# A transformer block on one core: the score matmuls of two pairs of heads grouped into three stretches in place of four

## What is computed

```python
x = x + 0.5 * ffn(layernorm(x), ...)      # shared + 8 routed SwiGLU experts, top 4, hidden size 341
x = x + attention(layernorm(x), W_qkv, W_out)   # 16 heads of 64, causal, 512 x 512 scores
x = x + 0.5 * ffn(layernorm(x), ...)

# attention
score = einsum("bihd,bjhd->bijh", q, k) / 64 ** 0.5
masked_score = score * mask + 1e30 * (mask - 1.0)      # mask = lower triangle
wmat = softmax(masked_score, axis=2)
out = einsum("bijh,bjhd->bihd", wmat, v).reshape(b, l, H * D) @ W_out
```

## Time and profile before

| | |
|---|---|
| median of 3 runs | 647.27 us (646.82 to 647.6) |
| the profiled execution | 647.71 us |
| its span, first to last instruction | 646.0 us |
| TensorE busy | 634.6 us (98%) |
| VectorE busy | 594.0 us (92%) |
| ScalarE busy | 563.2 us (87%) |
| GpSimd busy | 499.7 us (77%) |
| granted TensorE clock | 1.00 throughout |

### The profile page before, as it was taken

One profiled execution on the slowest core, in us unless ns is written; L12 is line 12 of the kernel. 1 busy time (PEld: TensorE's weight loads), 2 busy tenths in 40 slices (PEclk: granted clock), 3 DMA queues, 4 the chain that ended last, 5 costly groups with the idle time before them and its releaser, 6 DMA issues.

```text
span 646.0 us, 20994 instructions
## 1 busy us (share of the span) xinstructions
PE 634.6 (98%) x7860; PEld 419.2 (65%) x7860; DVE 594.0 (92%) x1654; ACT 563.2 (87%) x1092; POOL 499.7 (77%) x621
## 2 busy tenths in 40 slices
PE   7799999999999999999999999999999999999998
PEld 5476765666676576667657666766666666666665
DVE  4999789999999999999999999999999989789887
ACT  5999997999999899999889999998999997565655
POOL 4354686889899688999967889987898998473655
DMA  7900000689889186796746987772599776110000
GB/s 202 286 3 2 3 1 2 91 133 139 125 133 158 33 147 126 124 143 123 118 76 120 148 132 133 138 142 55 103 158 147 126 147 89 37 18 2 19 1 18
DMA packets 226489, 62.97 MB, mean 97 GB/s; under 512 B 213202, under 2 KB 225620, under 8 KB 226388
## 3 DMA queue, kind: packets, MB, share of 16 engines
q1 hardware_dynamic: 226388, 61.64, 54.6%
HBM read 7.87 MB, written 1.05 MB: 14 GB/s over the span
## 4 chain that ended last, share of the span: by engine, by line
PE 85%; DVE 10%; issue 2%; ACT 1%; DMA 1%; SPq 0%; DVEq 0%; ACTq 0%
PE bank L1185 25%; PE bank L1186 23%; PE bank L1187 23%; PE bank L1379 8%; PE bank L1342 4%; DVE probs L1884 2%; DVE glu L1788 2%; DVE glu L1793 2%; DVE xs L1823 1%; PE bank L1229 1%; DMA vl<-in_L_ffn_Ws 1%; PE bank L1277 0%; DVE ql L1599 0%; ACT glu L1525 0%; DVE vl L1599 0%
## 5 line engine op out<-in xcount | busy, mean ns | idle before, releaser
L1148 POOL TENSOR_TENSOR glul<-glu,gluh 128x512 f16<-128x512 f32 x191 | 218.6, 1165 | 80.8 <-ACT gluh L1546 80.5
L1152 POOL TENSOR_TENSOR paired<-probs,paired 128x512 f16<-128x512 f32 x160 | 184.4, 1164 | 28.4 <-ACT paired L1571 27.8
L1525 ACT ACTIVATE glu<-bank,tanh_scale 128x512 f32<-128x512 f32 x167 | 112.5, 679 | 38.4 <-PE bank L1187 36.4
L1563 ACT ACTIVATE probs<-probs,exp_bias 128x128 f32<-128x128 f32 (+3 forms) x256 | 130.4, 552 | 1.8 <-POOL exp_bias L1160 1.4
L1884 DVE CUSTOM_DVE_ANT_0 probs<-bank,causal,score_scale 128x128 f32<-128x128 f32 (+3 forms) x256 | 126.0, 544 | 1.5 <-POOL paired L1152 0.9
L1185 PE MATMUL bank<-w3h,gluh 128*128 128x128 f16 x708 | 124.2, 219 | 0.0
L1546 ACT ACTIVATE gluh<-glu 128x512 f16<-128x512 f32 x191 | 113.6, 621 | 12.0 <-DVE glu L1793 11.9
L1187 PE MATMUL bank<-w3h,glul 128*128 128x128 f16 x708 | 124.0, 219 | 0.0
L1186 PE MATMUL bank<-w3l,gluh 128*128 128x128 f16 x708 | 124.0, 219 | 0.0
L1788 DVE SCALAR_TENSOR_TENSOR glu<-glu,bank 128x512 f32<-128x512 f32 x167 | 113.3, 679 | 7.8 <-ACT glu L1525 7.4
L1793 DVE SCALAR_TENSOR_TENSOR glu<-glu,bank 128x512 f32<-128x512 f32 x167 | 114.7, 687 | 5.8
(11 more groups left out here) (227 smaller groups left out, 1611.5 us busy)
## 6 DMA issues: line engine op xcount, KB each, us to landing
pT<-paired SPq DMA_TRANSPOSE x160, 3.3
attention_raw<-in_L_attn_W_qkv SPq DMA_DIRECT2D x6, 256.0 KB, 5.1
xs<-in_L_attn_inputs SPq DMA_DIRECT2D x4, 256.0 KB, 4.4
vh<-in_L_ffn_W SPq DMA_DIRECT2D x6, 128.0 KB
pT<-in_L_ffn_W SPq DMA_DIRECT2D x6, 128.0 KB
out<-xs SPq DMA_DIRECT2D x3, 256.0 KB, 2.8
raw_more<-in_L_ffn_W SPq DMA_DIRECT2D x4, 128.0 KB
attention_raw<-in_L_attn_W_out SPq DMA_DIRECT2D x2, 256.0 KB, 6.3
```

Of the source, the lines that this page charges most:

```text
L1148: pool.tensor_tensor(glul[pair][:, :], g[:, :], gluh[pair][:, :], ALU.subtract).then_inc(glu_low)
L1152: pool.tensor_tensor(paired[n % PAIRED][:, 1, :], probs[n % PROBS][:, :], paired[n % PAIRED][:, 0, :], ALU.subtract).then_inc(probs_low)
L1525: act.activation(g[:, :], psum[b1.bank][:, :], ACT.Tanh, scale=tanh_scale[:, j:j + 1]).then_inc(tanh_made)
L1563: e = act.activation(pr[:, at:at + (qt + 1) * P], pr[:, at:at + (qt + 1) * P], ACT.Exp, bias=exp_bias[:, gp % 2, qt, head:head + 1], scale ...
```

## The change

The table of when scores are made now depends on whether the pair is even or odd. An even pair makes its steps 0 and 2 at its first unit step, and at its fifth its step 3 together with step 0 of the next pair. An odd pair makes its steps 2 and 3 at its third. So two pairs have three places with scores, each with two scores steps. The softening has a table of its own. Matmuls, tiles and instructions are the same in number and shape on every engine. All four `ORDER` strings are new throughout (every line differs); each has the same letters, each as often as before.

```diff
-SCORED_AT = {0: [0], 2: [2, 3]}
+SCORED_AT = [{0: [(0, 0), (0, 2)], 4: [(0, 3), (1, 0)]}, {2: [(0, 2), (0, 3)]}]
+SOFTENED_AT = [{0: [(0, 0), (0, 2)], 4: [(0, 3), (1, 0)]}, {2: [(0, 2)], 3: [(0, 3)]}]
...
         def scores(n):
-            gp, u = b * PAIRS + n // NU, n % NU
-            for of_unit in SCORED_AT.get(u, []) if 0 <= n < last else []:
+            p, u = n // NU, n % NU
+            for ahead_by, of_unit in SCORED_AT[p % 2].get(u, []) if 0 <= n < last else []:
+                gp = b * PAIRS + p + ahead_by
                 uses = [self.bank() for _ in range(2)]
...
-                    scored[b * last + n + of - u] = uses if len(units) == 1 else [uses[k]]
+                    scored[b * last + (p + ahead_by) * NU + of] = uses if len(units) == 1 else [uses[k]]
...
         def soften(n):
-            gp, u = b * PAIRS + n // NU, n % NU
-            if 0 <= n < last and u in SCORED:
-                tiles, units = SCORED[u]
-                units = [(b * last + n + of - u, of) for of in units]
+            p, u = n // NU, n % NU
+            for ahead_by, of_unit in SOFTENED_AT[p % 2].get(u, []) if 0 <= n < last else []:
+                gp = b * PAIRS + p + ahead_by
+                tiles, units = SCORED[of_unit]
+                units = [(b * last + (p + ahead_by) * NU + of, of) for of in units]
...
     "tensor": (
-        "FFBFFFFTzTFTTGNSgTNhhTTGSTTTThdThdhdhhGdTTShTdddhhdddTTTdhGThShTdTThdddRhdTTXhdhzdhTTddhgTdddhhhdhdd"
-        "hhhddddhhdhdhhxzhxdddkvhhvvddvhhqkhdqqhvdxqxkhwqqwhddwhvkwwqhdddwwqqhdvhwqkhwwwdxqqxvgwhwdhdwwqkhdww"
...
+        "FFTFzTFFFFBGNSgTTTNhhGTTSTThTTddTdhhGddhhSddTTTThhhTdddTdThGhhSTdThdTdTdddRhhXhzddTTdThhgddhTdhhhhhd"
+        "ddddddhhhhhhddxzhxdvkvdhhdvvddhhqqkhvddhqxqxhkddwqqhwvhwwddwqkqhwwhvdwqqkhhwwwddqqvwwgxxhhdwwdqqkhww"
...
```

More of the change, by code:

```diff
@@ L712 @@
     "gpsimd": (
[L713 to L717, removed]
@@ L718 @@
-        "ssssssssssssssfsssssssssssssssH"
+        "LLnLLLLsfLLssLEsssssnsEsssssssEsEsWWsWWYsssssssWWnsssfWWssssssssbbsnppbpbpppbsbppyppbbsuppbpsssbppps"
+        "sbubpsppssbbppupbppsbpfspbubsppppbssbnppupbbsspsppbybusspppssspsnuubssbypppbsspbppbsbspppbbssppupbps"
+        "sbpppubssbpppbbfuppppbsbssppubpssbpppbubsppnppbsssbpppybbsuppsspspnsssuybubsspppbbssspppbbpppbpbsspu"
+        "ppbbsppsfpsbupbsppbpsbpuppbssbppsspbubppppbbsspnuppbsssbpppbypusbpnssppssuybssbsuspppsfbbspppbbpsppb"
+        "spsbpupbpsppbsupbsbppsppbbusspppbssbpnbppsbuppbpspybpupbspsbppspsbbupsspppsssssussufssssssssnssyssss"
@@ L719 @@
+        "sssfssssssssssssssssssssssssssH"
     ),
     "tensor": (
-        "FFBFFFFTzTFTTGNSgTNhhTTGSTTTThdThdhdhhGdTTShTdddhhdddTTTdhGThShTdTThdddRhdTTXhdhzdhTTddhgTdddhhhdhdd"
-        "hhhddddhhdhdhhxzhxdddkvhhvvddvhhqkhdqqhvdxqxkhwqqwhddwhvkwwqhdddwwqqhdvhwqkhwwwdxqqxvgwhwdhdwwqkhdww"
-        "dqqwhwqkhdwwqwqhddwqhkwhwwxqxdwqhhdwwoqwhddwwqqhdhwhwwhdwhdhwwkvvvwwhxqxvdkhqqhvhddddkqohwqqhwwvhdww"
-        "qkhdwqqxgwvwwhxdwdqkhdddwwqqhvwhqwwkhwwddqqhhwwwxqxkhdwwqqhwhwddqkhwwddwqqhwowqhwddwqqhhxwwhwxhhwhwd"
@@ new lines @@
+        "ddddddhhhhhhddxzhxdvkvdhhdvvddhhqqkhvddhqxqxhkddwqqhwvhwwddwqkqhwwhvdwqqkhhwwwddqqvwwgxxhhdwwdqqkhww"
+        "whqqdddwwkhwwqqhwhwddqqkwhhwxwwxqqhdohwwdddwqqdhhwhwwwhddhhxkwwwxwvvvhwddvqqkhhdvqqhddkhowqqvwwhhdqq"
+        "kwwhvgdwwxqxhdqdwwwkhddwwqqhvhdwqwwkqhdhwwwqqdhwkhwwxqxqwhhwddwdwqqkdhhdwwwqqwohwddqqwhhwxwhhxwwhhdd"
+        "dkwwwhvvvvdwwdhqqkhhdvdqxqxkgohhwwdqqvwhddqqwwkhwwhvdwqqhwwdkhddwwwqqhvhwwxqqxkhwwhdwqqkdwwhdwhdwqqd"
+        "dhwwqqwkhwhdxwwqqxwwhohddqqwwwhhddhwdwhhhdwdwwkvvhvwvwxxqqkghhhdddvddqqkhowqqhwwvhwdqkwhqvhwdwwqxqxd"
@@ L729 @@
+        "whkwhwdwqqvhdwwwddqqkhwhhwdqqwwwdkhxqwhxqwwhddqqwwkhhddwwwqqhowdwhwdqqwhhwwdxghwwxdhhhwddhwddwwhhhdd"
+        "hhxhxdohhhhddddhddxhhhxddhddhhddhghdxhxdhhhddhhdhdhhddxhxddhdhhhddhhddhxhxddhhhhhhdddddxHxddd6"
     ),
     "scalar": (
-        "BlzCMMMNPPPPPNMhrhsPPPhssPPsPPhhMMshshAAhPPsAssshMMMhPsPPAsAhhPhAAPPssAAshPhsPPhlsshzQhPWZsshPPPWWhh"
-        "shrshsWshhhssWWWhhsshsslhhWzshskvhhssvvssvhhsskheeppshevpeespkpheeplephhsvpeypkehpeeupsshpevhpeeskph"
-        "pepsussephrvepephepskhepeupsseheppskheeppuhepepshsepkshepeeppuhshepesepplhyeupepsshephehpephhsusshss"
@@ L734 @@
[L734 to L738, removed]
@@ L739 @@
-        "hhhsshhshshlssyshhshssshhssshhhssshhhhssrhhhhssshhssshshsshhshssshhhhsssshhhsshhhsshsssH"
+        "lzCBMMMNPPPPNMhPhsrssPPPPhsPPMMhhsPshshAAAPPshsPhPhssMMMPsPAhhsAhAPshAAPPPAPsshlhhsWWzPPsZhsWPhhsPWh"
+        "hrssshhhssWsWWhhhWshsshlhQszshkvvsshhsvvhshssskheeevppphleepkhpeypeshpshevpepepkshuehpeeppvssehkphep"
+        "epesssvuprehepphsepsskehpuephsepepepkheepsuheppheeppksshheesppeuplsheephsspespyuephheepphsshehpshkss"
+        "suvvvhlsvyukehhpeepvphssekpehpepssepvehphepsekphvsepersuphepepekhpeepussphehvpepeukpeehhpepspsshepkh"
@@ new lines @@
+        "epeupseshhpepepeuskpheephsseppslephepepuehyshpehshpsepshsepshkhusvvvvlyhssukehheppvepssskeeepphhreps"
+        "psvehpepepkeehphupvepssshepepkhepeusshpvehpepepkehpehupepsskepephshsepeupehpepepkssehphueepsssplheep"
+        "hpepyepuhssepshheephushhplsyskvvhvvssskheeeusrhppvhpsskheeppeepsphepheepvkpeesvhhppuessspeehppkhuepe"
+        "sspvhepepepukheeshphpepsssekpheuphepseehpplepkyepehphuepssehpepepshueepsshhpeeeshppsprhhhssussshhhhu"
+        "sssshhhshsshhhsshsshhlhyssshhhsshhsssshrhhsshhshhhssshssshshhhshsshsshhhhsshhsshhhsssssH"
@@ L740 @@
     ),
     "vector": (
[L742 to L746, removed]
@@ L747 @@
-        "mmhhgiihrjhhchiccihhhhchhhhanchhhchhhchhchhchhhhgrjcchhhhchhhhccchhhDDDDhhhhchcchhhhhhHcccllllllllll"
-        "lM"
+        "nlMMGzSgPPPPUOOhGPhSrjUPPPPhMMMPPMMhhGchPhSUPPnchhhPMPPcGhPhSUhhPPPcPRhPXchhzPPchPhhPgchhrjhhhccnhhh"
+        "hhhzchkvvchhvvQchhmmnkhvmhmckhmmhhvcimimkhhcmvimhkihmmgrjvhcihmmkihcmihmckhimmhihmkminhhimmchhaimmch"
+        "hiichhhhnikcvvvhicvmmkhhmvmhkchammivhhmmkihvgrjcmhiimkhcmmhhviimmkchhmmhikihmcmhhiimmkcnhhimmcahimmh"
+        "hhichinhchikhvvvvichmmkhhvmmcgrkahjhmmvhimimkchhvmmicihkhmmhivhmimckhhimmkcihhmmchimmiknhhmincmahhmi"
@@ L749 @@
+        "imhchhichhihkvhvivvcmmkhgrjhcvhmmhkacmmhhimvkimvhhmnicmhikhmmvchiimmkhchhmimkimhhmichmkmichhmihmaich"
+        "mmhhigrihjhhhcciihchhhhhhcahhhccnhhhhcchhhhchhgrjchhhchhhhchhchhDDDDhhcchhhhhcchhhhhhcHcccMlllllllll"
+        "ll"
     ),
```

4 lines of the change are left out of this document (removed).

## The result

| | before | changed |
|---|---|---|
| median of 7 runs each | 646.89 us (646.82 to 647.6) | 649.01 us (648.57 to 649.8) |
| ratio of the runs | | 1.0028, 95% interval 1.0018 to 1.0038 |
| the profiled execution | 647.71 us | 648.81 us |
| its span | 646.0 us | 647.1 us |

I had predicted 645.5 us with a range of 643.9 to 648.3. The changed kernel is 2.1 us slower by the medians, and 1.1 us slower by the two profiled executions. That is 0.3%, small but clear of the scatter of the runs.

A forecast was written before the change was run, and what follows sets the result against it. TensorE, busy 98% of the span and almost never idle in attention, was taken as the bound. From 647.27 us, 2.3 saved at edges and 0.5 added for waits gave 645.5 us, range 643.9 to 648.3.

The forecast's parts named there:

- The edges: TensorE's switches between 128-row and 64-row matmuls in attention: 0.19 us per stretch, 88 stretches to 76, 2.3 us saved.
- The whole drain: Reading by record lengths: 0.16 us lost at each edge, 3.9 us saved in all, time 643.9; given no chance.
- the 64: Argument for the edge price: 64 scores steps of one shape cannot all meet the same wait; under 1.8 us excluded.
- +0.5 us for waits: Attention stage: allowance for TensorE's added waits, from probs-buffer waits and short stalls together.
- short stalls: TensorE between 87 and 560 us: some fifteen places, 2.3 us in sum, mostly at scores steps; change bounded -2.3 to +2.3.
- soften: VectorE's soften waiting for a probs buffer, nine tight places against two before; cost to TensorE between nothing and 2.7 us.
- The distances in TensorE's order: TensorE work between a step and the one needing its result, nearly all as long as before; costed at nothing.
- The start: New orders before attention: changes of 0.5 to 1 us either way, taken as 0 with bounds -1.2 and +1.2.
- The other signs: Profile signs: stage stalls above 4 us for rival 1, line 1152 waits some 2, TensorE busy about 2 us lower.
- rival 1: Attention stage: the new orders wait as much more as the edges save, +1.9 us, time 646.9; chance 0.32.
- Rival 2: VectorE becomes the bound through reused probs buffers, 32 waits; 649.7 at 0.4 us each, 651.3 at 0.45; chance 0.14.
- Rival 3: The new orders also remove present stalls, at the start or in the stage, 1.1 us more, time 643.9; chance 0.08.

The follow-up runs named there:

- e_split: Kernel before with 24 double scores stretches broken up by a weigh or down step put between the two scores steps; 652.33 us against 647.29, ratio 1.0071.
- p6_after: Changed kernel with six probs buffers in place of four, all orders the same; 649.45 us, ratio 1.0033 to the kernel before.
- lite runs: Both kernels, VectorE work left out: collects add 32 of 128 columns (before 0.9980, changed 0.9997), or hidden-tile products cover 256 of 512 (0.9976, 0.9987).
- a_again: The changed kernel unchanged, timed and profiled again beside the kernel before; 649.94 us against 647.17, ratio 1.0040.
- b_again: The kernel before, unchanged, run again for a second profile; 647.38 us against 647.32.
- f_merge2: Kernel before with nine local edits of TensorE's order that merge short scores and crossed down stretches, 88 to 80; 648.44 us against 647.40, ratio 1.0015.
- i_second_later: Changed kernel with, at seven stalled places, the step that follows the stretch put between its two scores steps; 654.4 us, ratio 1.0111 to before.
- g_later: Changed kernel with nine score stretches moved one step later in TensorE's order; 658.86 us, ratio 1.0178 to the kernel before.

## Why the prediction was wrong, point by point

- **The edges** (12 x 0.19 = 2.3 us): right in count, price and place; the trace has it at 152 changes, and e_split confirms it by the clock. The whole drain that the records suggested (0.16) is not what is paid. One argument was badly put: the 64 are places with scores before, which hold 96 scores steps of three shapes, not 64 of one shape.
- **The term that failed is the +0.5 us for waits.** I had the right place and the right releaser in the text: four banks are filled at every scores place, at a bank that VectorE has not yet emptied. I had bounds up to +2.3 for the short stalls and +2.7 for soften, and took +0.5 for both "nearer to the row of VectorE's present waits". It measured +3.1, more than the +2.3 that I had allowed the short stalls. The error was to take the row of VectorE's waits as the measure. VectorE waits hardly ever, in both kernels, because it is the engine being waited for. The row that bore on it was TensorE's own stall at 283.18, between two scores steps. But counting such places would not have given the size either. Stretches with two scores steps side by side went from 28 to 39, and 0.71 us times 39/28 is 0.3 us more. The stalls became more and above all longer, by the pairing and the new orders, and for that I had no measure.
- **The distances in TensorE's order** (scores to weigh, `pT`, hidden to down, q and k) were right to be costed at nothing: none shows in TensorE's waits. But they measure slack in one direction, from TensorE to its results. I had no such count for the other direction, from a bank's last reader to its next writer, which is where the stalls came up. Nor did I look for pairs of steps that wait for each other by the code: `xx` costs 0.23 each, seen nowhere before the change since the old order has none.
- **The start** (0, bounds 1.2 either way): 0.33 us by the traces, inside the bounds. My sign for it failed all the same: TensorE's idle time in the first 50 us was to stay within 1.2 us of 7.6 and is 9.6. In the changed kernel it waits 4.6 us in one piece for the first weights, with two single matmuls (the letter `F`) in front in place of six, and 1.7 for VectorE's weights. The 4.6 us cost nothing, since the first hidden matmul starts no later than with the old start. The 1.7 us stand at 28 us, in the part that takes 0.33 us longer.

```profile
PE bank L1232 <- DMA vl<-in_L_ffn_Ws: 4.6, 1, 4.6
PE bank L1188 <- DVE w1l L1602: 1.7, 1, 1.7
```

- **The other signs.** TensorE's stalls in the stage were to be above 4 us if rival 1 held: 5.6. VectorE's waits on line 1152 (now 1155) were to rise to some 2 us: 2.1. TensorE's busy time in the stage was to fall by about 2 us and fell by 1.0; that was a poor sign, since in a stretch of fixed length it tells only how much idle time the records leave.
- **Rival 1** (0.32) described what happened: new stalls eat the edges. Its price of 1.9 was too low: with 3.1 + 0.3 for the start the sum is 647.27 - 2.3 + 3.4 = 648.4, at the edge of my range, and the median lies another 0.6 us above, which no profile shows. **Rival 2**, the `probs` buffers, for which I gave the slower side its 0.14, is refuted: VectorE's waits there rose from 0.9 to 2.1 us only, and p6_after, which has 0.4, is no faster. The outcome was on its side by another mechanism. **Rival 3** did not occur.
- **The Trainium skill's rule** that tiling speeds up TensorE but not the emptying of PSUM (TensorEngine Tiling (Array Packing), Performance Considerations), which I had placed beside rival 2, belonged beside the main sum. The trace agrees in part: the lite runs show that a good half of the new stalls at second scores steps goes with VectorE's load. The same page, under Restrictions and Gotchas, says that different row tiles write to different PSUM banks. This kernel does so: a scores step takes one bank for each head, a double stretch four of the eight, and at 141.08 that meant 0.63 us of waiting; at the 13 places with step 2 behind step 0 it meant none.

**What stays open.** First, of the 3.1 us of new stalls about 2.5 remain with VectorE relieved of 56 us, and with more buffers as well. 0.46 of it are the two `xx` waits; the others must lie in the order of the lists and the handing out of banks, which no run separates, and I did not find one cause. No run has the new table with the old orders: from the code I expect them to block each other, since banks are given out along the list. So it is not shown whether the grouping itself costs anything, or only the new orders that came with it. That step 2 behind step 0 never stalls, and that the old pairing stalls longer than before, speaks for the orders. Whether better orders for the same table would have kept the 2.3 us is not known. Second, the medians differ by 2.1 and 2.8 us, the profiled executions by 1.1 and (a_again against b_again, on two chips) 1.8. In both pairs of profiles 1.0 to 1.2 us arise behind the 22nd hidden tile and 0.33 in the start; the rest of the difference between the profiles is scatter ahead of the first hidden matmul. The 0.6 to 1.4 us that the medians have beyond this are in no profile I have. Runs of the changed kernel scatter over 1.9 us (12 runs, 648.6 to 650.5), those of before over 1.4 (646.8 to 648.2, but for one of 652 and one of 723 us; f_merge2 has one of 923).

## What to carry to other kernels

When the busiest engine has no idle time, its next limit is the engine that frees its buffers; that engine shows almost no waits of its own, so look at the bottleneck's own stalls, by start-to-start distances. Their number alone is no forecast: here it would have given 0.3 us of the 3.1. Grouping steps to save a fixed cost at the edges makes them ask for their banks all at once: follow each kind of group in the lists and see when the last reader of each bank comes. Of the two new kinds here one never waited and one held the longest stalls. In a schedule where every engine's list is this tight, an edge of 0.19 us is worth saving only where nobody waits for the work: scores steps put one step later cost 0.7 to 1 us each (i_second_later, g_later), while 24 put one step earlier cost no more than their edges (e_split). And when a change gives every engine a new order, its effect and that of the new orders cannot be told apart afterwards.

## What the runs showed of the hardware that I had not expected

That the price of a change between matmuls of 128 rows and of 64 rows is one number: 0.095 us each way, for 65 to 512 columns on either side and both kinds of step, and paid in full on the path (48 changes more: 5.0 us more by the clock, 4.6 by the count). That a crossed down step that waits for the completion of the one right before it loses 0.23 us, at all eight places in the changed kernel and f_merge2 and more than two such changes. And that stalls repeat between executions, chips and even mixtures of kernels to about 0.01 us at nearly every place, except ahead of the first hidden matmul, behind the first loads: it starts anywhere from 18.0 to 19.9 us.
